# The centred residual computed once a step in fp32 and added to z by VectorE

## What is computed

```python
h = _layernorm(x) * (1 + cb) + sb                 # the "xt" of the experts
scores = xt @ gate_w                              # 8 experts, top 2, softmax -> wE
h = gelu(einsum('td,edf->etf', xt, w1) + b1)      # exact gelu, FF = 256
o = einsum('etf,efd->etd', h, w2) + b2
y = _layernorm(xt[None] + o, ln_g, ln_b)          # per token and expert
out = einsum('et,etd->td', wE, y)
x = x + gb * out
```

## Time and profile before

| | |
|---|---|
| median of 3 runs | 275.79 us (274.9 to 275.96) |
| the profiled execution | 275.96 us; its span 274.2 us |
| busy: PE, DVE, ACT, POOL | 239.3, 184.4, 159.8, 134.6 us |
| mean granted clock of PE | 0.966 of full speed |
| the chain that ended last | PE 48%, DVE 25%, ACT 15%, POOL 5%, issue 4% |
| a store of yout, issue to landing | 1.8 us (median of 8) |

### The profile page before, as it was taken

How to read it: one execution, slowest core, us unless ns; L and a number is a source line. 1 busy time by engine, 2 the same in 40 slices (tenths; PEclk the granted TensorE clock), 3 DMA queues, 4 the chain that set the end, 5 groups by cost and what they waited for, 6 DMA issues and landing times.

```text
span 274.2 us, 7792 instructions
## 1 busy us (share of the span) xinstructions
PE 239.3 (87%) x3064; PEld 206.0 (75%) x3064; DVE 184.4 (67%) x570; ACT 159.8 (58%) x419; POOL 134.6 (49%) x254
## 2 busy tenths in 40 slices
PE   7985884999999989998999989999999899989970
PEld 4653554988888878887888878888888788767960
DVE  2778469548596758666876769485967585456075
ACT  2354402784579375956487548844893769455650
POOL 8065436024670477146732675256714770468075
PEclk9979896899999999999999999999999999999996
DMA  6930000000000000000000000000000000000000
GB/s 203 332 151 0 2 4 1 0 4 2 4 19 2 4 2 0 19 6 0 4 19 2 2 2 20 4 4 2 19 2 2 2 1 19 6 0 0 22 0 20
DMA packets 5652, 6.23 MB, mean 23 GB/s; under 512 B 336, under 2 KB 5104, under 8 KB 5360
## 3 DMA queue, kind: packets, MB, share of 16 engines
q1 hardware_dynamic: 5616, 5.74, 6.5%
HBM read 4.68 MB, written 1.05 MB: 21 GB/s over the span
## 4 chain that ended last, share of the span: by engine, by line
PE 48%; DVE 25%; ACT 15%; POOL 5%; issue 4%; DMA 1%; POOLq 0%; ACTq 0%; DVEq 0%
ACT hid L484 10%; PE score L976 6%; PE z L1004 6%; PE turns L867 6%; DVE q_st L590 6%; PE score L968 5%; PE turns L869 3%; PE turns L868 3%; ACT L445 3%; DVE ypart L660 3%; PE score L987 3%; DVE xn L570 2%; PE score L1048 2%; POOL rstd L340 2%; PE turns L913 2%
## 5 line engine op out<-in xcount | busy, mean ns | idle before, releaser
L484 ACT ACTIVATE hid<-turns,pack_ffn 128x256 f32<-128x256 f32 x128 | 50.6, 472 | 44.4 <-PE turns L869 44.4
L1004 PEld LDWEIGHTS z<-w,hid 128*128 128x128 f32 x480 | 59.3, 191 | 3.7 <-issue 1.0
L1004 PE MATMUL z<-w,hid 128*128 128x128 f32 x480 | 61.5, 276 | 0.0
L867 PE MATMUL turns<-h_hi,w_hi 128*128 128x256 f32 x128 | 40.8, 318 | 8.4 <-ACT hid L484 4.4
L309 POOL TENSOR_SCALAR zvar<-zss 128x4 f32<-128x4 f32 x32 | 6.2, 193 | 82.1 <-DVE zss L646 73.1
L323 POOL TENSOR_TENSOR ypart<-ypart 128x256 f32<-128x256 f32 (+1 forms) x60 | 35.9, 599 | 18.4 <-DVE ypart L660 15.4
L869 PE MATMUL turns<-h_hi,w_lo 128*128 128x256 f32 x128 | 37.0, 289 | 0.0
L868 PE MATMUL turns<-h_lo,w_hi 128*128 128x256 f32 x128 | 36.9, 289 | 0.0
L660 DVE SCALAR_TENSOR_TENSOR ypart<-z,zcoef,ln_gG 128x128 f32<-128x128 f32 x120 | 34.1, 341 | 1.8 <-POOL zcoef L314 1.7
L867 PEld LDWEIGHTS turns<-h_hi,w_hi 128*128 128x128 f32 x128 | 25.1, 196 | 13.0 <-ACT hid L484 8.7
L310 POOL TENSOR_TENSOR zrstd<-zvar,mhalf 128x4 f32<-128x4 f32 x32 | 33.1, 1033 | 2.7
(11 more groups left out here) (143 smaller groups left out, 457.3 us busy)
## 6 DMA issues: line engine op xcount, KB each, us to landing
w<-in_w SPq DMA_DIRECT2D x2, 1024.0 KB, 9.3
out_x<-yout SPq DMA_DIRECT2D x8, 128.0 KB, 1.8
x_tokens<-in_x SPq DMA_DIRECT2D x1, 896.0 KB, 6.8
ln_g<-in_ln_g SPq DMA_DIRECT2D x1, 512.0 KB
pack_mod<-in_pack_mod SPq DMA_DIRECT2D x1, 385.0 KB, 3.0
pack_proj<-in_pack_proj SPq DMA_DIRECT2D x1, 193.0 KB, 4.7
pack_att<-in_pack_att SPq DMA_DIRECT2D x1, 130.5 KB, 4.6
x_tokens<-in_x SPq DMA_DIRECT2D x1, 128.0 KB, 3.0
```

Of the source, the lines that this page charges most:

```text
L484: last = a.activation(hid[:, e, c, :], U[(e + 1) % 2][:, c * STEP:(c + 1) * STEP], ACT.Gelu, bias=b1[:, e, c:c + 1])
L867: mm(outp, a_hi, b_hi, start=True, stop=False)
L1004: last = mm(z_bank(f, q)[:, e * D:(e + 1) * D], hid[:, ee, c, tt * P:(tt + 1) * P], w2[:, ee * CH + c, :], start=False, stop=e == HALF - 1 ...
```

## The change

- `center_r` is gone, and with it the two products with it in each quarter; the product with `ones_r` starts the group. PE now waits for `ones_done` once and, in each quarter, for `zx_s` in place of `u_done`.
- `gate` gains, for each tile, the product of h2T by `center` in fp32, 128 columns, into the other half of the bank.
- `take_gate` moves from DVE to ACT and copies, besides the scores, this centred residual to SBUF (`xc`, two steps of it).
- DVE gains `add_x`, four a step: zx = z + xc, 128x512, from PSUM and SBUF to SBUF, with xc broadcast over the four experts. `square`, `square_sum` and `scale` read `zx` in place of the bank.
- `scale(f, 2)` is no longer split around `take_gate`.

```diff
@@ -81,7 +81,8 @@
         b2_low = sb("b2_low", [EXPERTS, D], f32r)
         ln_g = sb("ln_g", [P, EXPERTS, D])
         ln_b = sb("ln_b", [EXPERTS, D])
-        center_r = sb("center_r", [P, D], f32r)
+        xc = sb("xc", [P, 2, TILES, D])
+        zx = sb("zx", [P, 2, HALF * D])
         rep16 = sb("rep16", [P, P], bf16)
         mask16 = sb("mask16", [P, 2, KEYS], bf16)
         ones = sb("ones", [P, P])
@@ -157,7 +158,7 @@
         loaded_att, loaded_mask, loaded_bo = sem("loaded_att"), sem("loaded_mask"), sem("loaded_bo")
         loaded_ffn, loaded_f, loaded_rest = sem("loaded_ffn"), sem("loaded_f"), sem("loaded_rest")
         loaded_w1, loaded_w2 = sem("loaded_w1"), sem("loaded_w2")
-        b2_moved = sem("b2_moved")
+        b2_moved, ones_done, zx_s = sem("b2_moved"), sem("ones_done"), sem("zx_s")
         ones_s, pad_s = sem("ones_s"), sem("pad_s")
         set_pool, set_act, set_pe = sem("set_pool"), sem("set_act"), sem("set_pe")
         set_vec, set_b2, set_att, silu_s = sem("set_vec"), sem("set_b2"), sem("set_att"), sem("silu_s")
@@ -451,10 +452,19 @@
                 a.activation(probT[:, s % 2, :], S[s][:, :], ACT.Copy).then_inc(p_out, 1)
 
             def square(f, q):
-                act.wait_ge(z_done, 4 * f + q + 1)
+                act.wait_ge(zx_s, 4 * f + q + 1)
                 if f > 0:
                     act.wait_ge(ss_s, 2 * f)
-                a.activation(zsq[:, q % 2, :], z_bank(f, q)[:, :], ACT.Square).then_inc(sq_s, 1)
+                a.activation(zsq[:, q % 2, :], zx[:, q % 2, :], ACT.Square).then_inc(sq_s, 1)
+
+            def take_gate(i):
+
+                act.wait_ge(gate_done, i + 1)
+                if i > 1:
+                    act.wait_ge(zx_s, 4 * (i - 1))
+                a.activation(gsc[:, :, :], U[0][:, 0:TILES * EXPERTS].rearrange("p (a e) -> p a e", e=EXPERTS), ACT.Copy)
+                a.activation(xc[:, i % 2, :, :], U[0][:, STEP:2 * STEP].rearrange("p (a d) -> p a d", d=D), ACT.Copy
+                             ).then_inc(g_out, 1)
 
             def exp_weight(f):
 
@@ -463,11 +473,11 @@
 
             def square_sum(f, q):
 
-                act.wait_ge(z_done, 4 * f + q + 1)
+                act.wait_ge(zx_s, 4 * f + q + 1)
                 if 4 * f + q - 1 > 0:
                     act.wait_ge(coef_s, 4 * f + q - 1)
                 for e in range(HALF):
-                    last = a.activation(zsq[:, q % 2, e * D:(e + 1) * D], z_bank(f, q)[:, e * D:(e + 1) * D], ACT.Square,
+                    last = a.activation(zsq[:, q % 2, e * D:(e + 1) * D], zx[:, q % 2, e * D:(e + 1) * D], ACT.Square,
                                         accum_out=zss[:, q % 2, e:e + 1])
                 last.then_inc(ss_act, 1)
 
@@ -491,8 +501,7 @@
                 take_k(n)
                 take_v(n)
                 act.wait_ge(loaded_ffn, 16)
-                a.activation(ones_r[:, :], ones[:, :], ACT.Copy)
-                a.activation(center_r[:, :], center[:, :], ACT.Copy)
+                a.activation(ones_r[:, :], ones[:, :], ACT.Copy).then_inc(ones_done, 1)
                 act.wait_ge(loaded_w1, 16)
                 a.activation(w1_hi[:, :, :, :], w1[:, :, :, :], ACT.Copy).then_inc(w1_hi_s, 1)
 
@@ -535,6 +544,7 @@
                 if ffn and att:
                     square_sum(f, 3)
                 if att:
+                    take_gate(i)
                     gelu(i, 0)
                     gelu(i, 1)
                     gelu(i, 2)
@@ -657,7 +667,7 @@
                         dve.wait_ge(lng_s, b + 1)
                 for e in range(HALF) if part is None else range(2 * part, 2 * part + 2):
                     ee = half * HALF + e
-                    last = v.scalar_tensor_tensor(ypart[:, tt, ee, :], z_bank(f, q)[:, e * D:(e + 1) * D],
+                    last = v.scalar_tensor_tensor(ypart[:, tt, ee, :], zx[:, q % 2, e * D:(e + 1) * D],
                                                   zcoef[:, q % 2, e:e + 1], ln_gG[:, b, ee, :], ALU.mult, ALU.mult)
                 if part != 0:
                     last.then_inc(u_done, 1)
@@ -676,11 +686,14 @@
                     v.tensor_tensor(yout[:, tt, :], ypart[:, tt, 0, :], X[:, TILES * f + tt, :],
                                     ALU.add).then_inc(y_s, 1)
 
-            def take_gate(i):
-
-                dve.wait_ge(gate_done, i + 1)
-                v.tensor_copy(gsc[:, :, :], U[0][:, 0:TILES * EXPERTS].rearrange("p (a e) -> p a e", e=EXPERTS)
-                              ).then_inc(g_out, 1)
+            def add_x(f, q):
+
+                dve.wait_ge(z_done, 4 * f + q + 1)
+                if 4 * f + q - 1 > 0:
+                    dve.wait_ge(u_done, 4 * f + q - 1)
+                v.tensor_tensor(zx[:, q % 2, :].rearrange("p (e d) -> p e d", d=D),
+                                z_bank(f, q)[:, :].rearrange("p (e d) -> p e d", d=D),
+                                bc(xc[:, f % 2, q % 2, :], 1, HALF), ALU.add).then_inc(zx_s, 1)
 
             def top_two(i):
 
@@ -810,12 +823,14 @@
                 n, f = i + 1, i - 1
                 if ffn and att:
                     weights(f)
+                    add_x(f, 0)
                     zsum(f, 0)
                     weights_T(f)
                 if nxt:
                     normed_front(n)
                 if ffn and att:
                     add_ln_b(f)
+                    add_x(f, 1)
                     scale(f, 0)
                     zsum(f, 1)
                 if nxt:
@@ -825,17 +840,17 @@
                 if att:
                     take_pv(i)
                     turn_attn(i)
+                if ffn and att:
+                    add_x(f, 2)
+                if att:
                     add_attn(i)
                     normed_second(i)
                     take_h2T(i)
                 if i == 0:
                     set_ffn_bias()
                 if ffn and att:
-                    scale(f, 2, 0)
-                if att:
-                    take_gate(i)
-                if ffn and att:
-                    scale(f, 2, 1)
+                    add_x(f, 3)
+                    scale(f, 2)
                 if att:
                     top_two(i)
                 if ffn and att:
@@ -1011,18 +1030,17 @@
                 if f == 0 and q == 0:
                     pe.wait_ge(w2_s, 4)
                     pe.wait_ge(b2_moved, 32)
+                    pe.wait_ge(ones_done, 1)
                 half, tt = q // 2, q % 2
                 pe.wait_ge(gelu_s, 8 * f + HALF * (half + 1))
                 if f == STEPS - 1 and q > 1:
                     pe.wait_ge(p_out, 4 * STEPS)
                 else:
                     if 4 * f + q - 1 > 0:
-                        pe.wait_ge(u_done, 4 * f + q - 1)
+                        pe.wait_ge(zx_s, 4 * f + q - 1)
                 bank, tok = z_bank(f, q), slice(tt * P, (tt + 1) * P)
                 by_e = bank[:, :].rearrange("p (e d) -> p e d", d=D)
-                mm(by_e, h2_hi[:, f % 2, tok], bc(center_r[:, :], 1, HALF), start=True, stop=False, skip_group_check=True)
-                mm(by_e, h2_lo[:, f % 2, tok], bc(center_r[:, :], 1, HALF), start=False, stop=False, skip_group_check=True)
-                mm(by_e, ones_r[:, :], b2_rows[:, half * HALF:(half + 1) * HALF, :], start=False, stop=False,
+                mm(by_e, ones_r[:, :], b2_rows[:, half * HALF:(half + 1) * HALF, :], start=True, stop=False,
                    skip_group_check=True)
 
             def turn_weights(f):
@@ -1066,7 +1084,9 @@
                 else:
                     pe.wait_ge(gelu_s, 8 * i)
                 for tt in range(TILES):
-                    last = mm(U[0][:, tt * EXPERTS:(tt + 1) * EXPERTS], h2T[:, tt * P:(tt + 1) * P], w_gate[:, :],
+                    mm(U[0][:, tt * EXPERTS:(tt + 1) * EXPERTS], h2T[:, tt * P:(tt + 1) * P], w_gate[:, :],
+                       start=True, stop=True)
+                    last = mm(U[0][:, STEP + tt * D:STEP + (tt + 1) * D], h2T[:, tt * P:(tt + 1) * P], center[:, :],
                               start=True, stop=True)
                 last.then_inc(gate_done, 1)
```

## The result

The changed kernel takes 285.97 us (median of 4 runs, 285.13 to 286.94), the kernel before beside it on the same chip 275.88. The ratio is 1.0379, 95% interval 1.0339 to 1.0419: slower, by 10.1 us. The forecast was 282.6 us, a range of 277 to 287, and a chance of 0.84 for slower. So sign and range held, and the point was 3.4 us low. The profiled run took 285.21 us, its span is 283.4. The ratios of this document leave out the runs that took over 1.5% more than the fastest of their kernel, so that a ratio is not the quotient of the two medians beside it.

What follows compares the result with a forecast made beforehand. No engine was taken as the bound; each stretch has its own chain of waits. Terms -5.05 (step 0), +0.65 (step 1), +6.3 (steps 1 to 6), +0.85 (step 7), +4.05 (end) sum to +6.8: 282.6 us, range 277 to 287.

Steps and rivals of the forecast that it cites:

- The gain of step 0: Step 0: with take_gate on ScalarE TensorE's stall goes and the last gelu ends at 49.13, not 54.18: -5.05 us.
- scale(1) and the port: Steps 1 to 6: scale(1), now with two SBUF inputs, waits out GpSimd's add_b_o, 0.57 us; with mask_q 0.6 a step.
- The quicker read from SBUF: VectorE's scale: if reading SBUF is quicker than PSUM, its four instructions save 0.2 us.
- The gate's products: Gate: two fp32 products of h2T by center precede the first expert in the chain, +0.45 us a step.
- expert 1 waits on its end, level with TensorE's own arrival. +0.45 stands: Gate: ScalarE's take_gate ends just as TensorE reaches expert 1, so nothing is added to the products' 0.45 us.
- Step 1: Start of step 1: VectorE's shifts end at 52.0, where weights could start at 51.2; put at +0.65 us.
- Step 7: Before step 7's first gelu: add_x(3), squares and take_gate come first, less 0.46 for down(0)'s pair; +0.85 us.
- The end: From the end of weights to the store: add_x, squares, coefficients and scale in line, 14.35 us against 10.32; +4.05.
- the third rival: TensorE's relief reaches the end: turn_x 0.46 us earlier each step, new work covered; -2.95, 272.8 us; chance 0.09.
- No port conflict: Rival: no port conflict and quick SBUF reads; steps cost 0.6 each, the end 0.4 less; +3.7, 279.5 us; chance 0.17.
- TensorE's relief reaches the end: Rival: turn_x moves 0.46 us earlier each step and new VectorE and gate work is covered; 272.8 us; chance 0.09.
- VectorE becomes the bound: Rival: scale(3) beside GpSimd's add_experts(2) grows 2.2 us, weights 1.05 late in steps 2 to 7; 289 us; chance 0.06.

Runs made afterwards that it cites:

- no_center: The kernel before without the two center_r products that begin each quarter of z, nothing in their place; 271.01 us, ratio 0.9865.
- gate_act: The kernel before with only take_gate (copying the gate's scores) moved from VectorE to ScalarE and scale(2) in one piece; 270.59 us, ratio 0.9808.
- bias_late: The kernel before with set_ffn_bias moved behind take_gate on VectorE in step 0; 270.69 us, ratio 0.9835.
- gate_dve: The changed kernel with both take_gate copies back on VectorE, between the halves of scale(2); 290.23 us, ratio 1.0548.
- bo_early: The changed kernel with GpSimd's add_b_o moved ahead of coefficients(1); 284.99 us, ratio 1.0296.
- psum_scale: The changed kernel with scale reading z from PSUM again in place of zx; 282.32 us, ratio 1.0295.
- products_only: The kernel before with take_gate on ScalarE, plus the fp32 h2T by center products and the xc copy, which nobody reads; 276.12 us, ratio 1.0051.
- adds_only: The changed kernel without the fp32 h2T by center products and the xc copy (xc holds zeros), VectorE's additions kept; 286.42 us, ratio 1.0386.
- twice: The changed kernel with the fp32 h2T by center products issued twice into the same place; 286.75 us, ratio 1.0428.
- norm_early: The changed kernel with normed_front(n) moved ahead of add_x(0) and zsum(0) on VectorE; 286.02 us, ratio 1.0421.

## Why the prediction was right, and where its sizes were off

- **Bound and direction** held (chain and VectorE's timeline of after). No engine is the bound, the one exposed pair of products is 0.46 a step (no_center: 0.47), and the additions on VectorE eat it ahead of turn_x: 0.03 is left as cost (forecast 0.04), with an idle time of 0.33 on TensorE (forecast 0.4 to 0.5). mask_q is 0.26 late (forecast 0.24).
- **The gain of step 0**, forecast 5.05, came out at 5.24 and belongs to the order of take_gate and set_ffn_bias alone (gate_act, bias_late, gate_dve). The 0.2 between the two is no finding, since the first gelu comes at a different time in each run; by the lengths of the gelus (12.80 and 7.38), less 0.44 for the gate's products, it is 4.98. The forecast let the clock stay up once the stall is gone; in the changed kernel and in gate_act it did, in one run of bias_late it did not.
- **scale(1) and the port.** Forecast 0.57 at most and 0.6 taken together with mask_q; measured 0.42 and 0.26, 0.68 together. bo_early and psum_scale give 0.40 and 0.46 back, so the cause is shown. The row that the forecast set beside it, the 2.18 us of the earlier trace rows, is a nearer relative than a like case: it has one tensor input, not two. The quicker read from SBUF, weighed at 0.2, does not exist: four scales alone take 1.13 from SBUF and 1.12 from PSUM.
- **The gate's products**: forecast +0.45, measured +0.44.
- **The step that failed** is "expert 1 waits on its end, level with TensorE's own arrival. +0.45 stands". It was not level. The four squares took 1.28 us, not the 1.0 of the forecast: from PSUM they had taken 1.14, and from zx each follows the last by 0.29 instead of 0.25. So g_out comes late, the second expert starts 0.13 later behind the first, and each gelu stretch is 0.20 longer. products_only has the same copies with no squares in their way: there the second expert is not late (0.80) and the gelus take 7.37, so that about 0.13 of the 0.20 is the squares'. Where the other 0.07 comes from no run tells. With 0.08 more for mask_q and scale(1), steps 2 to 6 took 1.32 and not 1.05: 1.35 of the missing 2.4 us.
- **Step 1**: forecast 0.65 over its neighbours, measured 0.55. **Step 7**: forecast 0.85, measured 1.19; its gelus took 9.26 as before (9.29), so the pair of down(0) between the experts gave nothing back there. no_center, whose gelus took 8.82 in that step, did get it, and so did gate_dve (8.86), so it is the place of the copies on ScalarE that took it away: the gate was done at 251.89, xc was out at 253.71.
- **The end**: forecast 4.05, measured 4.8 (15.09 less 10.32 is 4.77). Scale(3) and all behind coefficients(3) took 4.51, forecast 4.49. The 0.7 went in ahead of that, spread over links that were 0.1 to 0.2 longer each: squares(0) and squares(3) 1.28 and 1.24 instead of 1.1, coefficients(3) 1.73 instead of 1.65.
- Sum: forecast +6.8, measured +9.2 in the two profiles. The medians differ by 10.1. The rest goes with the clock: two of the four runs of the changed kernel had a mean of 0.95 and took 1.7 us more than the other two (0.97).
- **Slips of addition** in the forecast change little: step 7's four terms make 2.68, not 2.65; 14.35 less 10.32 is 4.03, not 4.05; the third rival's terms make -2.91, not -2.95; and 52.0 less 51.2, the price of step 1, is 0.8 and not 0.65.
- **Rivals.** "No port conflict" and "TensorE's relief reaches the end" are refuted. "VectorE becomes the bound": scale(3) of a step did grow (1.11 to 2.42 us), but `weights` started in time in step 4, 0.1 us after VectorE was through with its shifts (142.68 and 142.78), so its condition was not met. Beside additions of GpSimd the longest of the 128 scale instructions took 0.88 us, the median one 0.35; beside the power scale(0) took its usual 1.14 for four. The Trainium skill (SBUF — State Buffer, Who interferes with whom) states that a VectorE instruction with two SBUF inputs and a GpSimd one that reads SBUF exclude each other, each for its whole length: by that, the trace agrees for additions and not for the power.

## What to carry to other kernels

Taking work off the busiest engine is worth what lies on the chain, here one pair in four; ask of its replacement which queue it enters, and what stands behind it there. A copy that another engine waits for must not stand behind work that can wait: moving it alone gave 1.9%, where TensorE's relief with nothing paid for it (no_center) gave 1.4%. When an operand moves from PSUM to SBUF, count VectorE's SBUF inputs, and see which GpSimd instruction runs at that time; shifting that instruction helps only if its new place is free as well.

## What the runs showed of the hardware

- A VectorE cast with one SBUF input waited out a GpSimd multiply too. The cast of b2, 8x128, took 2.66 us in the kernel before and ended at 44.57; GpSimd's second multiply of 128x1024 ran from 42.16 to 44.49. In bias_late the cast took 0.38, begun 0.1 us after that multiply had ended. VectorE's timelines, before and bias_late:

```profile
41.91 2.66 DVE L557 CAST b_high<-b 8x128 fp32r<-8x128 f32 x1
```

```profile
43.88 0.38 DVE L557 CAST b_high<-b 8x128 fp32r<-8x128 f32 x1
```

- ScalarE's squares take longer from SBUF than from PSUM: those of 128x128 follow each other by 0.29 us and 0.25. The Trainium skill (VectorE: DVE Perf Modes, the TRN2 errata section) gives 43 ns as the difference, and the trace agrees; its 65 ns in favour of SBUF on VectorE the trace does not show (1.13 against 1.12 us for four).
- The granted clock fell to its lower level (0.50, 1.2 GHz) for 7 us in the middle of five of the fourteen profiled runs (bo_early and adds_only in step 3, twice in step 5, norm_early and gate_dve in step 6), and the step took 2.2 to 2.7 us more each time. All five are among the nine that have VectorE's additions; the five without them do not show it, gate_act for one, whose four runs all had a mean of 0.981 or more. With one profiled run of each, this is a pattern and nothing more. Why is open; no run was made to tell it.
